# A decoder layer on one core: who splits the second channels' queries of the cross attention in the last batch

## What is computed

```python
x = x + attn(layernorm(x), ...)                    # causal, 16 heads
def xattn(x_q, x_kv, ...):
    q = x_q @ W_q.T + b_q                          # x_q: 4 x 1024 x 256
    k = x_kv @ W_k.T + b_k                         # x_kv: 4 x 77 x 256
    v = x_kv @ W_v.T + b_v
    attn = softmax(heads(q) @ heads(k).T * 0.25)
    return merge(attn @ heads(v)) @ W_out.T + b_out
x = x + xattn(layernorm(x), ctx, ...)
x = x + ffn(layernorm(x), ...)                     # scales need the maximum over all tokens
```

## Time and profile before

| | us |
|---|---|
| median of 3 runs | 990.71 |
| lowest, highest | 989.15, 991.78 |
| the profiled execution, its own time | 986.81 |
| its span in the profile | 985.1 |

### The profile page before, as it was taken

How to read it: one execution, slowest core, us unless ns; L and a number is a source line. 1 busy time by engine, 2 the same in 40 slices (tenths; PEclk the granted TensorE clock), 3 DMA queues, 4 the chain that set the end, 5 groups by cost and what they waited for, 6 DMA issues and landing times. The chain is left out here.

```text
span 985.1 us, 17246 instructions
## 1 busy us (share of the span) xinstructions
PE 899.3 (91%) x6003; PEld 440.0 (45%) x6018; DVE 710.8 (72%) x1467; ACT 601.1 (61%) x1118; POOL 313.9 (32%) x348
## 2 busy tenths in 40 slices
PE   4788999999999989999999999999999998988976
PEld 2433443455544534464446343554444454543344
DVE  3889866768766783777777928777674568778977
ACT  2335577746576577447675775456788624637974
POOL 1351135330431218413431165313512122203723
PEclk9979999999999999999999999999999999999999
DMA  5340111335222142101220313202210243115009
GB/s 164 108 124 17 56 58 53 76 60 82 82 77 73 43 146 76 55 17 56 92 88 17 126 45 99 63 31 82 87 49 2 86 150 100 37 38 171 1 9 184
DMA packets 83568, 73.42 MB, mean 75 GB/s; under 512 B 19244, under 2 KB 79788, under 8 KB 83484
## 3 DMA queue, kind: packets, MB, share of 16 engines
q1 hardware_dynamic: 75772, 66.17, 22.2%
q0 software_dynamic: 4256, 3.21, 2.6%
q10 hardware_dynamic: 3456, 2.94, 1.0%
HBM read 19.81 MB, written 13.13 MB: 33 GB/s over the span
## 5 line engine op out<-in xcount | busy, mean ns | idle before, releaser
L767 ACT ACTIVATE probs<-psum 128x512 f32<-128x512 f32 (+1 forms) x608 | 314.6, 577 | 179.5 <-PE psum L962 176.6
L1136 DVE CUSTOM_DVE_ANT_0 junk<-psum,mask 128x640 bf16<-128x640 f32 (+3 forms) x256 | 253.4, 1022 | 59.4 <-PE psum L926 57.2
L684 POOL TENSOR_SCALAR_AFFINE_SELECT probs<-probs 128x512 f32<-128x512 f32 x128 | 81.6, 640 | 391.5 <-ACT probs L767 391.2
L962 PE MATMUL psum<-q_stack,k_stack 98*128 98x512 bf16 (+3 forms) x768 | 188.0, 331 | 6.7 <-DMA q_stack<-max_rows 2.6
L987 PE MATMUL psum<-probs,v_sb 128*17 128x512 f32 (+3 forms) x1536 | 158.9, 492 | 3.8 <-POOL probs L684 3.4
L1132 DVE TENSOR_REDUCE rowmax<-psum 128x4 f32<-128x512 f32 (+2 forms) x96 | 97.3, 1045 | 62.9 <-PE psum L920 62.5
L926 PE MATMUL psum<-k_stack,q_stack 96*128 96x512 bf16 (+3 forms) x512 | 128.7, 344 | 5.8 <-DVE rowmax L1136 4.5
L962 PEld LDWEIGHTS psum<-q_stack,k_stack 98*128 98x128 bf16 x768 | 62.7, 98 | 136.6 <-ACT probs L767 80.9
L886 PE MATMUL psum<-xnT,wT 128*128 128x512 f32 x192 | 90.8, 604 | 0.6 <-ACT xnT L732 0.5
L811 PE MATMUL psum<-wT,xnT 128*128 128x256 f32 x384 | 87.6, 385 | 0.4 <-ACT xnT L732 0.3
L811 PEld LDWEIGHTS psum<-wT,xnT 128*128 128x128 f32 x384 | 73.3, 193 | 12.6 <-ACT xnT L732 1.2
(11 more groups left out here) (180 smaller groups left out, 1242.7 us busy)
## 6 DMA issues: line engine op xcount, KB each, us to landing
q_stack<-q_parts SPq DMA_DIRECT2D x192, 64.0 KB, 2.6
k_stack<-k_parts SPq DMA_DIRECT2D x192, 64.0 KB, 2.6
xq_stack<-xq_parts SPq DMA_DIRECT2D x168, 64.0 KB, 2.6
xn<-in_x SPq DMA_DIRECT2D x8, 512.0 KB, 5.0
res<-in_x SPq DMA_DIRECT2D x4, 1024.0 KB, 6.8
out<-res SPq DMA_DIRECT2D x8, 512.0 KB, 2.9
normT_hbm<-xnT SPq DMA_DIRECT2D x6, 512.0 KB, 3.9
xf<-normT_hbm SPq DMA_DIRECT2D x6, 512.0 KB, 3.7
```

The costliest lines, as they stand in the source:

```text
L684: nc.gpsimd.affine_select(out=tile, in_=tile, compare_op=ALU.is_ge, fill=0.0, base=0, pattern=[[0, GH], [1, P]], channel_multiplier=-1).th ...
L767: nc.scalar.activation(probs[n % 2][:, heads * k:heads * k + heads, 0:cols], bank_a(s)[:, 0:heads * cols].rearrange("p (h n) -> p h n", h= ...
L962: last = nc.tensor.matmul(bank[:, cols * n:cols * n + cols], k_stack[:, slot, h, P * j:P * j + P], q_stack[:, slot, half, h, q0 - HALF * h ...
L1136: nc.vector.tensor_tensor_reduce(out=junk[D_STEPS.place(s) % 2][:, 0:keys], in0=bank_d(s)[:, 0:keys], in1=m.mask[:, T - keys:T], scale=1.0 ...
```

## The change

`quick` now names the second channels' pieces of the last batch too, so that VectorE does their three operations and GpSimd has none of them. ScalarE gets one wait, since both channel halves of a token half use the same `junk` tile:

```diff
 def quick(s):
-    return s[1:4] in ((0, 0, 0), (1, B - 1, 0))
+    return s[1:4] == (0, 0, 0) or s[1:3] == (1, B - 1)
...
                         if quick(s):
                             act.wait_ge(*d_emptied(("s1", B - 1, G - 1, s1_of(BOTH)[-1])))
+                            if c:
+                                act.wait_ge(quick_low, QUICKS.upto(("q", 1, b, 0, half)))
                         bias = m.bias_t[:, 2, c:c + 1]
```

## The result

Median of 20 runs: 996.08 us with the change, 991.91 without. Ratio 1.0037, 95% interval 1.0020 to 1.0054: slower by 0.37%, some 3.7 us. The forecast was 3.4 us slower, 994.1 in a range of 991.2 to 996.2. The difference is close to the forecast; the level, 996.08, is just inside the range, because the forecast started from a median of 3 runs (990.71) that 17 more runs moved to 991.91.

The account below looks back on a forecast made before the run. From 823 us the program's end hangs on VectorE, in a ladder of maxima, transposes and scores with TensorE. Terms -0.1 + 2.5 + 1.0 = +3.4 us on the 990.71 median gave 994.1 us, range 991.2 to 996.2.

Parts of the forecast that it names:

- First added piece: Channel 1, first half, on VectorE: paid by shorter normalisations, weights start at 814.17 instead of 814.25; -0.1 us.
- Case C: The four normalisations of xn stay long without GpSimd: +4.3, with the clock +5.3 us, 995.0 to 996.0; chance 0.10.
- E: Faster: freed normalisations let TensorE begin up to 2 us sooner at 814; -1 us, chance 0.03.
- Second added piece: Channel 1, second half: VectorE works and stands for ScalarE's copies, so the maxima come late; +2.4 us against 823.17.
- GpSimd and SyncE's queue at nothing: GpSimd loses six instructions before its first shift, and all pieces are ready in time for SyncE's queue; cost nothing.
- Case D: No slower: SyncE's queued copies lead the ladder and VectorE's delay vanishes; 0 to 0.5 us, 991.0, chance 0.12.
- The clock: TensorE's wait for maxima grows from 2.06 to about 4.4 us, lowering its clock: +1.0 us, between 0 and 1.7.
- A: The forecast: 2.4 us on the ladder and a lower clock in it, 2.6 to 4.2 us; chance 0.50.
- B: The ladder's delay without the lower clock: +2.4 us, 993.1 us; chance 0.25.
- The sum: Whole kernel: -0.1 + 2.5 + 1.0 = +3.4 us, nothing behind takes it up, up to the feed-forward part.

Follow-up runs that it names:

- first_half: Against the kernel before, only the first token half's second-channel piece goes to VectorE, the other stays with GpSimd; ratio 0.9987 (0.9961 to 1.0013).
- own_tile: The changed kernel, but VectorE's two new pieces keep their remainder in rem tiles of their own instead of junk; ratio to the kernel before 1.0013.
- pool_both: Kernel before plus two waits: GpSimd's first piece starts after the four normalisations, its second after VectorE's piece of channel half 0; ratio 0.9983, again 0.9971.
- second_half: Against the kernel before, only the second token half's second-channel piece goes to VectorE; ratio 1.0037 (1.0010 to 1.0064).
- pool_both_fill: pool_both with 15 instead of 24 filler matmuls ahead of the second token half's transposes; ratio to the kernel before 0.9991.
- lean: pool_both_fill with three of six gate weight steps and both weight transposes moved behind maxima of the ladder; ratio to the kernel before 0.9975.
- more_fill: The changed kernel with 20 instead of 6 filler matmuls ahead of the transpose of head group 0's negated maxima; ratio to the kernel before 1.0025.

## Why the prediction was right

**First added piece.** Forecast -0.1 us with the weights at 814.17, that is 5.12 from the zero; measured 5.09. `first_half` shows it alone. The pitch of the undisturbed normalisations, 1.29 us by the first half's rows, came as 1.30 in `own_tile` and `pool_both`; in the change itself it is covered by the wait for ScalarE's copy, which came as forecast (the piece starts at 3.30, forecast 3.32). Case C (they stay long) fell, and so did E: the transposes start at 5.33 as before.

**Second added piece.** Forecast +2.5, and both together +2.4, with the maxima at 16.51; measured 16.47. Its parts: VectorE's stand forecast between the pieces, 1.4 to 1.5, measured 1.41; the last operation back at 0.69. `own_tile` and `second_half` took the term apart as worked out.

**GpSimd and SyncE's queue at nothing.** GpSimd's first shift followed the maxima in step, and TensorE's longest wait for a row DMA in the whole stage was 0.3 us in the first profile of the change and 0.6 in the second. SyncE's queue did not lead in the changed kernel. Case D fell: the delay did not shrink down the ladder. Its mechanism is real, though: it shows in `pool_both_fill` and `lean`, where the scores that wait for the copies come 1.1 and 1.3 us sooner than before the change.

**The clock.** Forecast +1.0 from bounds of 0 and 1.7; measured 0.84, 1.02 and 0.96 in three profiles, removed by fillers in `more_fill`. So A held and B did not. That the size came so close is partly luck: it was picked between bounds of 0 and 1.7, the upper one from a stretch (L1353, the feed-forward part's second product) where TensorE alone leads. The reason for a fall at all, a stand longer than the ones before, was an argument; three profiles out of three with the fall, and the one in which fillers cut the stand to 1.39 us without it, are what shows it.

**The sum.** From the zero to the last maxima the two profiles of the change took 3.05 and 3.50 us more than the one before; forecast 3.4. `more_fill`, without the fall, took 2.07 more. The whole, 3.7 with an interval of 2.0 to 5.4, agrees. That the profile of the change shows 6.1 us more up to the feed-forward part was not foreseen: two more falls of the clock lie in it, here one window of each:

```profile
866.00:869.00 3.00, 2.29 (x9) 1.62 (x10) 2.76 (x11) 1.26 (x4) 1.01 (x2) 0.71 0.03 3
...
885.00:888.00 3.00, 3.00 (x15) 2.47 (x14) 2.86 (x6) 1.57 (x3) 0.00 (x0) 0.55 0.00 0
```

They are not of the change: `first_half`, whose ladder begins as before, has falls near the same two places, some 4.5 and 21.5 us behind its last maxima (its feed-forward part starts at 80.72), `own_tile` and the second profile of the change none there.

## What to carry to other kernels

An engine's own time for a piece of work does not tell what it costs to move it there. Here 3.6 us of VectorE's work made the maxima 2.35 us later, and 0.63 us later without the one shared scratch tile (`own_tile`); the long stand then cost about 1 us more by TensorE's clock. Where a helper takes over a second piece that uses the same scratch, look which producer now waits for the first piece to be done.

Where two engines stretch each other's instructions, delaying the one that has slack by a semaphore can beat moving its work: in this kernel two waits won about 0.2%, and the move lost 0.37%. Before that, look at what leads next. Here it was ScalarE's copy, then the weights, then TensorE's own work and SyncE's queue, and each took a part of the gain.

## What the runs showed of the hardware

Beside a GpSimd `tensor_tensor`, VectorE's `tensor_scalar` from SBUF took 1.10 instead of 0.35 us, and a two-input `tensor_tensor` 1.53 instead of 0.69. Small ones are not spared: beside a GpSimd copy of 0.61 us, a 128x16 `tensor_scalar` took 0.55 instead of 0.17. The strongest case lies in the kernel before, and in all the others too, at the last maxima of the ladder. VectorE's negation there, GpSimd's addition beside it, and TensorE's wait for it:

```profile
851.84 2.33 DVE L1151 TENSOR_SCALAR negmax<-rowmax 128x16 bf16<-128x16 f32 x1
```

```profile
849.45 4.67 POOL L679 TENSOR_TENSOR res<-res,bias_f 128x1024 f32<-128x1024 f32 x2
```

```profile
854.42 0.23 PE L949 MATMUL psum<-identb,negmax 128*32 128x128 bf16 x1 [1.20 <-DVE negmax L1152]
```

2.33 us instead of 0.17, until GpSimd's second addition ends, and TensorE stands 1.20 us for it. No run here holds that addition back; it is the next thing to try.

A reduction over 1280 elements took 1.48 us either way. The Trainium skill, "SBUF — State Buffer", § Who interferes with whom, says of `tensor_reduce` on trn2 that it never contends; the rows of `pool_both` agree.

Which stand lowers TensorE's clock is not told by its length alone: a stand of 2.78 us in `own_tile` and one of 3.76 us before 31.56 kept it, 1.96 us before 954.48 lost it. Such falls at different places go with the scatter of one kernel's runs: of the changed kernel's, the shortest, 989.55 us, had a mean granted clock of 0.987, and one of 1000.68 us had 0.973. Among the runs of one kernel, a mean clock lower by 0.001 goes with about 0.8 us more (an estimate from all the runs' times and clocks). A difference of 3 us between two single runs of this kernel says nothing. Counted from a shared event, the stretch up to the first maxima repeats to 0.02 us; the last maxima repeated to 0.06 us in `pool_both` and to 0.45 in the change.
